# DLRM tower: the turns of gathered rows on VectorE in two pieces of 256 batch columns

## The chip, the cores and the metric

The kernel runs on one core of one Trainium2 chip. The metric is the device time in microseconds (us), from the start of the program on the core to its end. Engines go by the profile's names: PE (TensorE), PEld (its weight loads), DVE (VectorE), ACT (ScalarE), POOL (GpSimd) and SP (SyncE, which issues DMAs here).

## What is computed

For 512 samples, 40 embedding rows of 32 numbers each are looked up; each of the 780 pairs of fields gives one bilinear number; these and 16 dense numbers go through a three-layer perceptron.

```python
e = jnp.stack([tbl_0[ids[:, 0]], ..., tbl_39[ids[:, 39]]], axis=1)   # (512, 40, 32)
xi = inputs[:, iidx, :]          # inputs is e; iidx, jidx = triu_indices(40, k=1)
xj = inputs[:, jidx, :]
out = jnp.einsum('bpd,pde,bpe->bp', xi, bilinear_matrices, xj)      # z, (512, 780)
h = jnp.concatenate([z, dense_ctx], axis=1)
h = jnp.maximum(h @ W_top1 + b_top1, 0.0)    # 796 -> 512
h = jnp.maximum(h @ W_top2 + b_top2, 0.0)    # 512 -> 256
y = h @ W_top3                               # (512, 1)
```

## The kernel before

The fields stand in ten groups of four. A group's embeddings lie in `xt[:, t, :]` with the batch along the free dimension: 4 fields x 32 numbers on 128 partitions, 512 batch columns. They come there in two ways. Four groups (`HOT_POS` = 0, 1, 3, 5) have small tables; PE picks their rows by one-hot matmuls in the first 35 us. The other six (`GATHER_POS` = 2, 4, 6, 7, 8, 9) are gathered by GpSimd: sixteen indirect DMAs a group, each for 32 samples, into `x_rows[:, g, c, :]`, batch along the partitions. A **turn** is the 32x32 block transpose on DVE (L498) that makes `xt[:, t, :]` from `x_rows[:, g]`. It waits for the group's gathers on `gathered[g]` and counts `turned`; PE, DVE and SP wait for a group by that count (`x_there`), and ScalarE waits for the fourth turn before it reuses the first columns of `x_rows`.

The pairs are worked off in 49 **units**, k = 0 to 48 (`UNIT[k] = (t, u)`). A unit is

- on PE, four fp32 matmuls (L564, eight records in the trace) of 32 rows each, which form y = M x in four PSUM banks. They run as two pairs. Each pair takes one of three slots of two banks (`Y_SLOTS` = 3) and waits (`prod_done`) until DVE has read what stood in it: for the first pair of unit k that is product 2 of unit k-2, for the second pair product 1 of unit k-1;
- on DVE, two **products** of 128x1024 elements (L517), y times the partner's embeddings. Product 1 reads the first pair of banks, product 2 the second. Each waits for `y_done`; product 1 of the later units for `sum_done` too, and where t = u for the rearranged rows of `mix_pieces` (`mixed`), which SP moves inside SBUF;
- on PE again, two units later, the **sum** (L635): four matmuls that add each product over its 32 numbers into `z_ps`. Eight units fill a block, which ScalarE copies to `z_t`.

From unit 11 on PE also works at the first layer: one **first-layer half** (L534) of 256 columns a unit, two in units 17, 23, 31 and 39 and none in the units after these. The order on PE within a unit is: the unit's matmuls, the sum of unit k-2, the first-layer half. ScalarE and GpSimd take the results out and add them. After the last unit come the last block's layer, the second and the third layer.

The order of the work is written out in tables. `AFTER["turn"] = [1, 10, 17, 23, 31, 39]` says ahead of which unit's products DVE does each turn; in the code before, a turn stands whole ahead of product 1 of that unit. `LATE_SUMS` puts off the sums of units 0 to 8, so that in unit 10 PE has two sums (7 and 8) and in units 3 to 9 the sum of unit k-3.

Of the kernel before, what the change touches and what calls it, by code (L numbers as in the profile page):

```python
# [44 lines left out]
GATHER_POS = [t for t in range(GROUPS) if t not in HOT_POS]  # L45
GATHERS = len(GATHER_POS)
CHUNKS = BATCH // DIM

# [38 lines left out]
def partner(t, u, s):  # L89

    if t != u:
        return t
    if t % 2 == 0 and s == FREE_ROW[t // 2]:
        return SPLIT[0] if t > 0 else t
    if t % 2 == 1 and s == G - 1:
        return t ^ 1
    return mix_slot(t, s)
# [12 lines left out]
def mix_pieces(g):  # L110

    pieces = []
    for s in range(G):
        if leaves(g, s) is None or (g % 2 == 1 and s == G - 1):
            continue
        for jj, (source, q) in enumerate(leaves(g, s)):
            if jj > 0 and pieces[-1][2] == source and pieces[-1][3] + pieces[-1][4] == q:
                pieces[-1][4] += 1
            else:
                pieces.append([mix_slot(g, s), jj, source, q, 1])  # L120
    return pieces
# [32 lines left out]
L1_HALF = BATCH // 2  # L154
# [8 lines left out]
AFTER = {  # L163
    "l1": sorted([*(k for k in range(11, UNITS) if k - 1 not in TURN_STEPS), *TURN_STEPS, 45, 48]),
    "turn": [1, 10, 17, 23, 31, 39],
}


def place_of(k):
# [36 lines left out]
def bass_dlrm_tower(nc, ids, rows, hot_ids, numbers, negatives, hot_tables, dense, mats, w1, b1, w2, b2, w3, select, out):  # L206
    steps = schedule()

    def x_there(engine, t):

        if t in HOT_POS:
            engine.wait_ge(x_out, 2 * HOT_POS.index(t) + 2)
        else:
            engine.wait_ge(turned, GATHER_POS.index(t) + 1)
# [4 lines left out]
    with ExitStack() as ctx:  # L219
        def sb(name, shape, dt=F32):  # L220
            return ctx.enter_context(nc.sbuf_tensor(name, shape, dt))
# [4 lines left out]
        def sem(name):  # L226
            return ctx.enter_context(nc.semaphore(name))

        ids_sb = sb("ids_sb", [P, 2, GATHERS * CHUNKS], I32)
        row = sb("row", [P, GATHERS * CHUNKS], I32)  # L230
        x_rows = sb("x_rows", [P, GATHERS, CHUNKS, DIM])
        xt = sb("xt", [P, GROUPS + 3 * 2 * MIX_RING, BATCH])
# [32 lines left out]
        def ones(j):  # L265

            if j in BY_SCALAR:
                n = 2 * (scalar_rounds.index(j) % ONES_RING)
                return z_t[:, 1 + n:3 + n, :].rearrange("p b c -> p (b c)").bitcast(BF16).rearrange(
                    "p (f c) -> p f c", f=G)  # L270
            return hot[:, vector_rounds.index(j) % HOT_RING, :, :]
# [29 lines left out]
        w1_rest_in = sem("w1_rest_in")  # L301
        head_in = sem("head_in")
        w2_in = sem("w2_in")
        gathered = [sem(f"gathered{g}") for g in range(GATHERS)]
        mats_in = [sem(f"mats_in{c}") for c in range(len(MAT_CHUNKS))]
        plane_done = [sem(f"plane_done{o}") for o in range(HOTS)]
        hot_done = sem("hot_done")
# [1 line left out]
        turned = sem("turned")  # L309
# [21 lines left out]
        @block.gpsimd  # L331
        def _(pool):
            pool.wait_ge(ids_in, 16)
            nc.gpsimd.tensor_tensor(row[:], ids_sb[:, 0, :], ids_sb[:, 1, :], ALU.add).then_inc(row_done, 1)
            pool.wait_ge(row_done, 1)
            for g in range(GATHERS):
                for c in range(CHUNKS):
                    n = g * CHUNKS + c
                    pool.indirect_dma_start(out=x_rows[:, g, c, :], out_offset=None, in_=rows,  # L339
                                            in_offset=bass.IndirectOffsetOnAxis(ap=row[:, n:n + 1], axis=0)  # L340
                                            ).then_inc(gathered[g], 16)
            for n, (b, m) in enumerate(L1_STEP):
                if b > 1:
                    pool.wait_ge(t_out, n + 1)
                    if b > 2:
                        pool.wait_ge(joined, L1_STEP.index((b - 1, m)) - M1 + 1)
                    nc.gpsimd.tensor_tensor(h1[:, m, :], part_sb[b][:, m * BATCH:(m + 1) * BATCH], h1[:, m, :],  # L347
                                            ALU.add).then_inc(joined, 1)
# [131 lines left out]
        @block.vector  # L480
        def _(dve):
            nc.vector.memset(prod[:, 0, 0, :], 0.0).then_inc(cleared, 1)  # L482
            dve.wait_ge(number_in, 16)
            for k in range(len(ROUND)):
                o, r = ROUND[k]
                if r == 0:
                    dve.wait_ge(hot_id_in[o], 16)
                if k not in BY_SCALAR:
                    n = vector_rounds.index(k)
                    if n >= HOT_RING:  # L490
                        dve.wait_ge(hot_used, vector_rounds[n - HOT_RING] + 1)
                    nc.vector.tensor_scalar(ones(k).rearrange("p f b -> p (f b)"), hot_id[:, o, :],  # L492
                                            number[:, o, r:r + 1], None, ALU.is_equal).then_inc(hot_done, 1)
            for k in range(UNITS):
                for g in [g for g, before in enumerate(AFTER["turn"]) if before == k]:
                    t = GATHER_POS[g]
                    dve.wait_ge(gathered[g], 16 * CHUNKS)
                    nc.vector.transpose(xt[:, t, :], x_rows[:, g, :, :].rearrange("p c d -> p (c d)")).then_inc(turned, 1)  # L498
                t, u = UNIT[k]
                if u != t and all(v == w or v != t for v, w in UNIT[:k]):  # L500
                    x_there(dve, t)
                if u == t:
                    dve.wait_ge(mixed[t], 16 * len(mix_pieces(t)))
                    x_there(dve, t ^ 1)
                    if t % 2 == 0 and t > 0:
                        x_there(dve, SPLIT[0])
                    pairs = [sorted(partner(t, u, s) for s in (2 * half, 2 * half + 1)) for half in range(2)]
                    partners = [xt[:, low:high + 1:high - low, :] for low, high in pairs]
                else:
                    partners = [xt[:, t, :].unsqueeze(1).to_broadcast([P, 2, BATCH])] * 2  # L510
                for half in range(2):
                    slot = (2 * k + half) % Y_SLOTS
                    dve.wait_ge(y_done, 2 * k + half + 1)
                    if half == 0 and k >= PROD_UNITS:

                        dve.wait_ge(sum_done, k - PROD_UNITS + 1)
                    nc.vector.tensor_tensor(prod[:, k % PROD_UNITS, 2 * half:2 * half + 2, :],  # L517
                                            y_ps[:, 2 * slot:2 * slot + 2, :], partners[half],
                                            ALU.mult).then_inc(prod_done, 1)
            dve.wait_ge(sum_done, UNITS)  # L520
            nc.vector.tensor_copy(z_t[:, BLOCKS - 1, :], z_ps[:]).then_inc(z_last, 1)
            for m in range(M1):
                dve.wait_ge(joined, L1_STEP.index((BLOCKS - 2, m)) - M1 + 1)
                dve.wait_ge(l1_done, m + 1)
                nc.vector.tensor_tensor(h1[:, m, :], y_ps[:, LATE_BANK[m], :], h1[:, m, :], ALU.add).then_inc(l1_added, 1)

        @block.tensor
        def _(pe):
# [17 lines left out]
            def first_steps(k):  # L546

                nonlocal chunks_seen
                t, u = UNIT[k]
                if MAT0[chunks_seen] <= k:  # L550
                    pe.wait_ge(mats_in[chunks_seen], 16)
                    chunks_seen += 1
                if all(w != u for _, w in UNIT[:k]):
                    x_there(pe, u)
                for s in range(G):
                    half = 2 * k + s // 2
                    slot = half % Y_SLOTS
                    if s % 2 == 0 and half >= Y_SLOTS:

                        pe.wait_ge(prod_done, half - Y_SLOTS + 1)  # L560
                    elif s % 2 == 0:
                        pe.wait_ge(x_out, 2 * half + 2)
                    rows = slice(s * DIM, (s + 1) * DIM)
                    last = nc.tensor.matmul(y_ps[:, 2 * slot + place(t, u, s) % 2, :], m_sb[rows, k, :], xt[rows, moving(t, u, s), :],  # L564
                                            start=True, stop=True)
                    if s % 2 == 1:
                        last.then_inc(y_done, 1)
# [178 lines left out]
```

## Time and profile before

| | us |
|---|---|
| median of 3 runs | 171.64 (171.23 to 171.9) |
| the profiled execution | 171.2 |
| its span | 169.4 |
| PE busy | 164.5 (97%) |
| DVE busy | 145.0 (86%) |
| POOL busy | 112.8 (67%) |
| ACT busy | 42.8 (25%) |

The span is the time from the first to the last instruction of the profiled execution; 1.8 us of that execution lie around it. A row of the timeline gives start, duration, engine, line, operation, tiles and how many instructions follow each other without a gap; the bracket gives the idle time ahead and what ended it. PE's matmuls overlap, so in the chain of waits a group counts from where the one ahead of it ended. The granted clock of TensorE is at full speed throughout the span (1.00 in the mean).

### The profile page before, as it was taken

What the parts mean: (1) busy time and instruction counts of PE and PEld (TensorE: products, weight loads), DVE (VectorE), ACT (ScalarE), POOL (GpSimd) and SP (SyncE); (2) the same over time, 40 slices, a digit from 0 to 9 for tenths busy, and PEclk for the clock granted to TensorE, in tenths of its full rate; (3) what the DMA queues carried; (4) which work ended last, traced back from release to release, by engine and by line L of the source; (5) the groups of instructions that cost most, each with busy time, mean ns of one, the idle gap of its engine ahead of it and who ended that gap; (6) DMA issues with size and microseconds to landing.
All of it is one profiled execution on the core that took longest, in us unless ns stands there. A gap on an engine that the chain in (4) does not pass through costs nothing.

```text
span 169.4 us, 3937 instructions
## 1 busy us (share of the span) xinstructions
PE 164.5 (97%) x1670; PEld 53.0 (31%) x1670; DVE 145.0 (86%) x144; ACT 42.8 (25%) x56; POOL 112.8 (67%) x117
## 2 busy tenths in 40 slices
PE   6999999999999999999999999999999999999993
PEld 2334444332232223333232223332323323232220
DVE  1799999999999999999999899998999999793500
ACT  3389995120000011130020210202111021111503
POOL 3777777777777777777777777777799993333000
PEclk9999999999999999999999999999999999999999
DMA  5999156987998570100026611000003450000000
GB/s 134 374 423 376 30 151 201 316 245 220 307 360 276 153 220 16 15 12 16 16 52 179 174 23 16 16 14 13 16 12 93 119 164 2 4 0 0 4 0 0
DMA packets 12890, 20.15 MB, mean 119 GB/s; under 512 B 3924, under 2 KB 6872, under 8 KB 12744
## 3 DMA queue, kind: packets, MB, share of 16 engines
q1 hardware_dynamic: 9144, 18.03, 32.7%
q0 software_dynamic: 3072, 1.58, 5.7%
q10 hardware_dynamic: 656, 0.28, 0.6%
q8 instruction: 13, 0.21, 0.5%
q14 instruction: 5, 0.04, 0.1%
HBM read 11.92 MB, written 0.00 MB: 70 GB/s over the span
## 4 chain that ended last, share of the span: by engine, by line
PE 87%; ACT 4%; DMA 4%; issue 2%; SPq 1%
PE y_ps L564 33%; PE z_ps L635 29%; PE t_ps L534 10%; PE y_ps L534 6%; DMA table<-hot_tables 4%; PE y_ps L578 4%; PE t_ps L578 3%; ACT plane L414 2%; PE z_ps L578 1%; ACT z_t L424 1%; PE y_ps L543 1%; SPq L356 1%; ACT xt L433 0%; ACT hot_id L475 0%; ACT xt L435 0%
## 5 line engine op out<-in xcount | busy, mean ns | idle before, releaser
L517 DVE TENSOR_TENSOR prod<-y_ps,xt 128x1024 f32<-128x1024 f32 x98 | 114.4, 1217 | 6.2 <-PE y_ps L564 3.2
L339 POOL DMA_INDIRECT x_rows<-rows,row x96 | 92.3, 961 | 29.2 <-issue 28.9
L564 PE MATMUL y_ps<-xt,m_sb 32*128 32x512 f32 x392 | 60.0, 640 | 0.0
L635 PE MATMUL z_ps<-prod,sel 128*32 128x512 f32 x392 | 51.8, 604 | 0.0
L564 PEld LDWEIGHTS y_ps<-xt,m_sb 32*128 32x128 f32 x392 | 19.1, 182 | 25.7 <-issue 16.7
L492 DVE TENSOR_SCALAR hot<-hot_id,number 128x2048 bf16<-128x2048 int16 x34 | 22.9, 749 | 4.2 <-DMA hot_id<-hot_ids 4.1
L534 PE MATMUL t_ps<-z_t,table 128*32 128x256 f32 x320 | 23.5, 379 | 0.0
L635 PEld LDWEIGHTS z_ps<-prod,sel 128*32 128x32 f32 x392 | 7.9, 107 | 36.3 <-DVE prod L517 17.3
L534 PEld LDWEIGHTS t_ps<-z_t,table 128*32 128x32 f32 x320 | 10.4, 110 | 21.4 <-issue 20.4
L578 PE MATMUL y_ps<-hot,plane 128*32 128x512 bf16 x200 | 15.1, 379 | 0.4 <-ACT plane L414 0.4
L461 ACT ACTIVATE z_t<-z_ps 128x512 f32<-128x512 f32 x6 | 3.6, 597 | 38.9 <-PE z_ps L635 38.9
L347 POOL TENSOR_TENSOR hot_id<-x_rows,hot_id 128x512 f32<-128x512 f32 x4 | 5.1, 1274 | 9.8 <-ACT x_rows L458 9.8
L458 ACT ACTIVATE hot<-t_ps 128x512 f32<-128x512 f32 x8 | 4.8, 596 | 22.7 <-PE t_ps L534 22.7
L414 ACT ACTIVATE plane<-table 128x512 bf16<-128x512 uint8 (+2 forms) x10 | 9.1, 966 | 3.9 <-DMA table<-hot_tables 3.9
L347 POOL TENSOR_TENSOR hot_id<-hot,hot_id 128x512 f32<-128x512 f32 x8 | 9.9, 1273 | 0.0
L578 PE MATMUL y_ps<-hot,table 128*32 128x512 bf16 x100 | 9.7, 383 | 0.2 <-DVE hot L492 0.2
L534 PE MATMUL y_ps<-hot_id,w_sb 128*32 128x512 f32 x64 | 7.0, 592 | 0.0
L572 PE MATMUL y_ps<-prod 128*128 128x512 bf16 x14 | 5.5, 576 | 1.5 <-DVE prod L482 1.5
L578 PEld LDWEIGHTS y_ps<-hot,plane 128*32 128x32 bf16 x200 | 5.2, 97 | 4.8 <-ACT plane L414 0.9
L454 ACT ACTIVATE hot_id<-t_ps,b_sb 128x512 f32<-128x512 f32 x4 | 2.7, 687 | 15.4 <-PE t_ps L534 15.4
L458 ACT ACTIVATE x_rows<-t_ps 128x512 f32<-128x512 f32 x4 | 2.4, 597 | 13.5 <-PE t_ps L534 13.5
L578 PE MATMUL t_ps<-hot,plane 128*32 128x512 bf16 x72 | 5.3, 380 | 0.0
(41 smaller groups left out, 58.5 us busy)
## 6 DMA issues: line engine op xcount, KB each, us to landing
xt<-xt SPq DMA_DIRECT2D x18, 192.0 KB, 2.5
xt<-xt SPq DMA_DIRECT2D x17, 128.0 KB, 2.4
hot_id<-hot_ids SPq DMA_DIRECT2D x4, 512.0 KB, 6.0
xt<-xt SPq DMA_DIRECT2D x32, 64.0 KB, 2.3
x_rows<-rows,row POOLq DMA_INDIRECT x96, 2.4
table<-hot_tables SPq DMA_DIRECT2D x2, 640.0 KB, 8.5
table<-w SPq DMA_DIRECT2D x1, 1280.0 KB
table<-hot_tables SPq DMA_DIRECT2D x2, 512.0 KB, 6.0
```

The lines of the kernel that those rows point to most:

```text
L339: pool.indirect_dma_start(out=x_rows[:, g, c, :], out_offset=None, in_=rows, in_offset=bass.IndirectOffsetOnAxis(ap=row[:, n:n + 1], axis= ...
L347: nc.gpsimd.tensor_tensor(h1[:, m, :], part_sb[b][:, m * BATCH:(m + 1) * BATCH], h1[:, m, :], ALU.add).then_inc(joined, 1)
L414: nc.scalar.activation(plane[:, o % PIECE_RING, byte, :, cols], low_byte(table[:, o, :, :], byte)[:, :, cols], ACT.Copy, scale=256.0 if by ...
L458: nc.scalar.activation(part_sb[b][:, m * BATCH:(m + 1) * BATCH], t_ps[:], ACT.Copy).then_inc(t_out, 1)
L461: nc.scalar.activation(z_t[:, k, :], z_ps[:], ACT.Copy).then_inc(z_out, 1)
L492: nc.vector.tensor_scalar(ones(k).rearrange("p f b -> p (f b)"), hot_id[:, o, :], number[:, o, r:r + 1], None, ALU.is_equal).then_inc(hot_ ...
L517: nc.vector.tensor_tensor(prod[:, k % PROD_UNITS, 2 * half:2 * half + 2, :], y_ps[:, 2 * slot:2 * slot + 2, :], partners[half], ALU.mult). ...
L534: last = nc.tensor.matmul(bank[q * DIM:(q + 1) * DIM, :], weights[:, q * DIM:(q + 1) * DIM], columns, start=start, stop=stop, skip_group_c ...
L564: last = nc.tensor.matmul(y_ps[:, 2 * slot + place(t, u, s) % 2, :], m_sb[rows, k, :], xt[rows, moving(t, u, s), :], start=True, stop=True)
L572: nc.tensor.matmul(y_ps[:, 0, :], zeros[:, BATCH:BATCH + P], zeros[:, 0:BATCH], start=True, stop=True)
L578: done = nc.tensor.matmul(bank[f * DIM:(f + 1) * DIM, :], piece[:, f, r * DIM:(r + 1) * DIM], ones(j)[:, f, :], start=first, stop=last, sk ...
L635: last = nc.tensor.matmul(z_ps[s * DIM:(s + 1) * DIM, :], window, prod[:, k % PROD_UNITS, place(*UNIT[k], s), :], start=first, stop=(k == ...
```

## The change

Each turn is cut into two pieces of 256 columns. The gathers of a group count on two semaphores, one for its first eight and one for its last eight, and each piece waits for its own. The second piece stands where the turn stood; the first stands one unit earlier, except in the turn ahead of unit 1, whose two pieces both stand there. `turned` is counted by the second piece alone.

```diff
+HALF_CHUNKS = CHUNKS // 2
...
+TURN_BEFORE = {}
+for g, k in enumerate(AFTER["turn"]):
+    for half in range(2):
+        TURN_BEFORE.setdefault(k - (half == 0 and k > 1), []).append((g, half))
...
-        gathered = [sem(f"gathered{g}") for g in range(GATHERS)]
+        gathered = [[sem(f"gathered{g}_{half}") for half in range(2)] for g in range(GATHERS)]
...
-                                            ).then_inc(gathered[g], 16)
+                                            ).then_inc(gathered[g][c // HALF_CHUNKS], 16)
...
-                for g in [g for g, before in enumerate(AFTER["turn"]) if before == k]:
-                    t = GATHER_POS[g]
-                    dve.wait_ge(gathered[g], 16 * CHUNKS)
-                    nc.vector.transpose(xt[:, t, :], x_rows[:, g, :, :].rearrange("p c d -> p (c d)")).then_inc(turned, 1)
+                for g, half in TURN_BEFORE.get(k, []):
+                    chunks = slice(half * HALF_CHUNKS, (half + 1) * HALF_CHUNKS)
+                    dve.wait_ge(gathered[g][half], 16 * HALF_CHUNKS)
+                    turn = nc.vector.transpose(xt[:, GATHER_POS[g], half * L1_HALF:(half + 1) * L1_HALF],
+                                               x_rows[:, g, chunks, :].rearrange("p c d -> p (c d)"))
+                    if half == 1:
+                        turn.then_inc(turned, 1)
```

`L1_HALF` is 256. Nothing else is changed; the other engines have the same instructions in the same order.

On DVE, units 9 and 10 before (L517 the products, L498 the turn):

```order
L517 TENSOR_TENSOR prod<-y_ps,xt 128x1024 [waits sum_done,y_done]
L517 TENSOR_TENSOR prod<-y_ps,xt 128x1024 [waits y_done]
L498 STREAM_TRANSPOSE xt<-x_rows 128x512 [waits gathered1]
L517 TENSOR_TENSOR prod<-y_ps,xt 128x1024 [waits sum_done,y_done]
L517 TENSOR_TENSOR prod<-y_ps,xt 128x1024 [waits y_done]
```

The same place after (L526 the products, L504 the turn's pieces; `gathered1_0` and `gathered1_1` are the semaphores of its first and last eight gathers):

```order
L504 STREAM_TRANSPOSE xt<-x_rows 128x256 [waits gathered1_0]
L526 TENSOR_TENSOR prod<-y_ps,xt 128x1024 [waits sum_done,y_done]
L526 TENSOR_TENSOR prod<-y_ps,xt 128x1024 [waits y_done]
L504 STREAM_TRANSPOSE xt<-x_rows 128x256 [waits gathered1_1]
L526 TENSOR_TENSOR prod<-y_ps,xt 128x1024 [waits sum_done,y_done]
L526 TENSOR_TENSOR prod<-y_ps,xt 128x1024 [waits y_done]
```

The turn stood between the products of unit 9 and those of unit 10; a first piece now stands ahead of unit 9's.

On DVE, units 16 and 17 before; unit 16 is one with t = u, whose product 1 has four waits:

```order
L517 TENSOR_TENSOR prod<-y_ps,xt 128x1024 [waits y_done,sum_done,turned,mixed5]
L517 TENSOR_TENSOR prod<-y_ps,xt 128x1024 [waits y_done]
L498 STREAM_TRANSPOSE xt<-x_rows 128x512 [waits gathered2]
L517 TENSOR_TENSOR prod<-y_ps,xt 128x1024 [waits sum_done,y_done,turned]
L517 TENSOR_TENSOR prod<-y_ps,xt 128x1024 [waits y_done]
```

The same place after:

```order
L504 STREAM_TRANSPOSE xt<-x_rows 128x256 [waits gathered2_0]
L526 TENSOR_TENSOR prod<-y_ps,xt 128x1024 [waits y_done,sum_done,turned,mixed5]
L526 TENSOR_TENSOR prod<-y_ps,xt 128x1024 [waits y_done]
L504 STREAM_TRANSPOSE xt<-x_rows 128x256 [waits gathered2_1]
L526 TENSOR_TENSOR prod<-y_ps,xt 128x1024 [waits sum_done,y_done,turned]
L526 TENSOR_TENSOR prod<-y_ps,xt 128x1024 [waits y_done]
```

Again one piece has moved ahead of the two products of the unit before, unit 16. The products that follow the pieces wait for the same semaphores as before.

## Rows read from the trace of the kernel before

**Rows 1.** busy by stretch: window, us, busy (count) of PE, PEld, DVE, ACT, POOL
```profile
55.00:152.00 97.00, 97.00 (x924) 29.80 (x920) 91.12 (x81) 14.06 (x24) 71.52 (x71) 1.00 0.23 59
```

**Rows 2.** chain of waits, 52 to 60 us: start us, us, what
```profile
52.76 1.85 PE z_ps L635 x16
54.61 1.07 PE y_ps L564 x8
...
57.11 1.07 PE y_ps L564 x8
58.18 1.00 PE z_ps L635 x8
59.18 0.43 PE t_ps L534 x8
```

**Rows 3.** timeline, DVE, 50.5 to 56: start, us, what, count [idle before]
```profile
50.36 2.34 DVE L517 TENSOR_TENSOR prod<-y_ps,xt 128x1024 f32<-128x1024 f32 x2
52.62 0.70 DVE L498 STREAM_TRANSPOSE xt<-x_rows 128x512 f32<-128x512 f32 x1
53.25 2.31 DVE L517 TENSOR_TENSOR prod<-y_ps,xt 128x1024 f32<-128x1024 f32 x2
55.77 1.22 DVE L517 TENSOR_TENSOR prod<-y_ps,xt 128x1024 f32<-128x1024 f32 x1 [0.21 <-issue]
```

**Rows 4.** timeline, DVE, 65.9 to 75, read in four pieces
```profile
65.90 2.36 DVE L517 TENSOR_TENSOR prod<-y_ps,xt 128x1024 f32<-128x1024 f32 x2 [0.34 <-PE y_ps L564]
68.38 2.35 DVE L517 TENSOR_TENSOR prod<-y_ps,xt 128x1024 f32<-128x1024 f32 x2
70.65 0.70 DVE L498 STREAM_TRANSPOSE xt<-x_rows 128x512 f32<-128x512 f32 x1
71.38 2.36 DVE L517 TENSOR_TENSOR prod<-y_ps,xt 128x1024 f32<-128x1024 f32 x2
73.77 1.23 DVE L517 TENSOR_TENSOR prod<-y_ps,xt 128x1024 f32<-128x1024 f32 x1
```

**Rows 5.** timeline, PE, L564 of units 10, 17 and 18
```profile
51.42 1.33 PE L564 MATMUL y_ps<-xt,m_sb 32*128 32x512 f32 x8
...
69.67 1.14 PE L564 MATMUL y_ps<-xt,m_sb 32*128 32x512 f32 x8
...
72.60 1.20 PE L564 MATMUL y_ps<-xt,m_sb 32*128 32x512 f32 x8
```

**Rows 6.** chain of waits, 69 to 94 us
```profile
69.74 1.07 PE y_ps L564 x8
...
74.79 1.39 PE y_ps L564 x8
...
77.61 1.07 PE y_ps L564 x8
...
85.10 1.07 PE y_ps L564 x8
...
93.12 1.07 PE y_ps L564 x8
```

**Rows 7.** groups by line: count | busy us, mean ns | idle before, releaser
```profile
L517 DVE TENSOR_TENSOR prod<-y_ps,xt 128x1024 f32<-128x1024 f32 x98 | 114.4, 1217 | 6.2 <-PE y_ps L564 3.2 <-issue 0.2
L339 POOL DMA_INDIRECT x_rows<-rows,row x96 | 92.3, 961 | 29.2 <-issue 28.9 <-POOL row L334 0.3
...
L498 DVE STREAM_TRANSPOSE xt<-x_rows 128x512 f32<-128x512 f32 x6 | 4.2, 703 | 0.2 <-DMA x_rows<-rows,row 0.2
```

**Rows 8.** groups by form, DVE: the products of 512 columns
```profile
L525 DVE TENSOR_TENSOR hot_id<-y_ps,hot_id 128x512 f32<-128x512 f32 x4 | 2.8, 692 | 1.9 <-PE y_ps L534 1.9
```

**Rows 9.** timeline, DVE, 28 to 34: the product after the first turn
```profile
31.81 2.36 DVE L517 TENSOR_TENSOR prod<-y_ps,xt 128x1024 f32<-128x1024 f32 x2 [0.15 <-PE y_ps L564]
```

**Rows 10.** timeline, DVE, 82.5 to 87.2: the fourth turn
```profile
86.28 0.71 DVE L498 STREAM_TRANSPOSE xt<-x_rows 128x512 f32<-128x512 f32 x1 [0.22 <-DMA x_rows<-rows,row]
```

## The prediction

> **What bounds the kernel now.** I read the busy times by stretch first, then the chain of waits, then the timelines of VectorE (DVE) and TensorE (PE) around the turns. From 55 to 152 us PE is busy for all 97.0 us and DVE for 91.1 [rows 1]. There the chain consists of PE rows alone: a unit's first matmuls (L564) 1.07, a sum (L635) 1.00, a first-layer half (L534) 0.43, so 2.50 us from one unit to the next [rows 2]. I write U(k) for the L564 group of unit k; the one that the chain has at 54.61 is U(11), at 57.11 U(12), at 69.74 U(17).
>
> Two loops matter. The first is DVE's own pitch: the two products of a unit last 2.34 to 2.36 together and one lasts 1.21 to 1.23 [rows 3, 4], so they start 1.13 to 1.14 apart, so a unit costs DVE 2.27 against PE's 2.50, and DVE has 0.23 free per unit. The second is narrower. The second pair of matmuls in U(k+1) needs the PSUM banks that product 1 of unit k reads. One place shows it: U(10) starts at 51.42 and lasts 1.33, where the undisturbed U(17) lasts 1.14 [rows 5]; its second pair started 0.19 late, at 51.61, and product 1 of unit 9 ended at 51.57 (50.36 plus 1.21 [rows 3]). So PE goes on about 0.05 after that product's end. Round this loop: product 1 of a unit starts 1.17 after the unit's matmuls do (unit 18: 72.60 in PE's timeline, 73.77 in DVE's [rows 4, 5]), it takes 1.23, the release 0.05: 2.45. Against 2.50 that is 0.05 of slack. Where a unit has no first-layer half (unit 18, PE needs 2.07) the loop itself holds PE for 0.3 to 0.4: U(19) lasts 1.39 in the chain, 0.32 over 1.07 [rows 6]. Where a unit has two such halves (17, 23, 31, 39, just where the turns stand) PE needs 2.93, and 0.48 of delay on DVE is free.
>
> **What the change does, part by part.** Six turns of 0.70 [rows 7] become twelve pieces of 256 columns. A 1024-column product takes 1217 ns and a 512-column one 692 [rows 7, 8], so 512 columns are 525 ns and a piece is 703 minus 262, 0.44 us. In engine time: a whole turn takes 0.63 from its start to the next start where the next product doesn't wait for it (52.62 to 53.25 [rows 3]) and 0.73 where it does (70.65 to 71.38 [rows 4]). A piece then takes 0.37 and 0.47. Together 0.84 for 0.73: DVE does 0.1 more per turn. Bounds: the cheapest piece is half a turn with no fixed part (0.28 and 0.38), the dearest costs what a whole one does (0.63 and 0.73). I take 0.37 and 0.47, since the 512- and 1024-column rows show both slope and fixed part.
>
> The Trainium skill (VectorE: DVE Perf Modes, section "The TRN2 errata — SBUF-src ops pay a fixed extra latency per instruction") says that an SBUF-source operation pays a fixed extra cost per instruction, and gives about 151 cycles at 0.96 GHz for fp32; it advises tiles of 512 elements or more. By it a piece is (256 + 151)/0.96, an estimate of 0.42 us, and each added instruction costs 0.16; all six on the path would be 0.9, and the kernel at 172.6. The rows give a similar fixed part (692 minus 525 ns), but the price here is set by place, as follows.
>
> Turn before unit 1 (both pieces stay there): 0.1 more on DVE, which idled 0.15 behind this turn until PE's group for the next product was there [rows 9]. Cover: just that 0.15. Cost 0, at most 0.1.
>
> Turn before unit 10: its first piece now stands ahead of product 1 of unit 9. Up to here DVE runs without a gap, and U(10) waits for just that product [rows 3, 5]. The product ends 0.37 later, and with it U(10). Behind U(10) stand two sums and U(11) without a wait (52.76, 1.85, then 54.61 [rows 2]), so PE is 0.37 late from then on. Before, the whole turn cost nothing: it lay beside these two sums, and DVE even idled 0.21 before 55.77 [rows 3]. Smaller work on DVE there gives nothing back. **+0.37**.
>
> Turn before unit 17: the first piece goes ahead of product 1 of unit 16. Product 2 of unit 15 starts at 67.05 (65.90 plus 1.14), so the piece starts at 68.18 and product 1 of unit 16 at 68.55, not 68.38 [rows 4]; PE's second pair in U(17) comes at 68.55 + 1.23 + 0.05 = 69.83 where it came with the first at 69.67 [rows 5]. **+0.16**. The second piece leaves product 1 of unit 17 at about 71.28, 0.1 earlier, but PE reaches U(18) only after the two first-layer halves. What that takes away is the 0.06 by which U(18) lasted longer than U(17) [rows 5], and nothing comes of it: the next link, from U(18)'s start to U(19)'s second pair, is the 2.45 loop, which begins at PE's own start and not at the turn's end. Before unit 31 the same (unit 30 too is of the kind with several waits): **+0.16**.
>
> Turn before unit 39: unit 38 is a plain one, in the 2.50 rhythm. Of the piece's 0.37 DVE's free 0.23 hides the most; product 1 starts 0.14 late, and the loop becomes 2.45 + 0.14 = 2.59 against 2.50. **+0.09**.
>
> Turn before unit 23: the same +0.09, but here the turn waited 0.22 for its last gather [rows 10], and from U(23) to U(26) it took 8.02 (85.10 to 93.12), from U(17) to U(20) 7.87 (69.74 to 77.61 [rows 6]). With everything before 0.53 late, DVE comes to the second piece after the gather has landed, so 0.15 comes back. **-0.06**.
>
> The semaphore per piece does nothing more: the first eight gathers of a group land some 10 us before the last eight (GpSimd takes 0.96 and 0.30 of idle time for each of the 96 [rows 7], eight are 10 us). Only the second piece counts `turned`, so PE, SP and ScalarE wait for the same point as before; SP's moves after the turn of unit 10 come at most 0.1 later relative to DVE, and their use is a dozen microseconds off. What queues behind each first piece is only DVE's products, and behind them PE.
>
> Sum: 0.37 + 0.16 - 0.06 + 0.16 + 0.09 = **0.72 us**, all in PE's chain, and from unit 40 to the end nothing can take it back. The profiled execution took 171.2 (span 169.4 and 1.8 around it); it would take 171.9. It is 0.4 under the median of the runs shown, 171.64; on that the forecast is 172.3. With the cheap bound the same working gives 0.28 + 0.07 - 0.15 + 0.07 + 0 = 0.3 (171.9), with the dear one 0.63 + 0.49 + 0.27 + 0.49 + 0.42 = 2.3 (173.9).
>
> **Rivals.** (a) *The stall behind each turn goes.* Smaller pieces would leave DVE never more than half a turn behind, and U(18), U(19) and their three fellows would last 1.07. They are 0.37 over it per turn [rows 5, 6], so 4 x 0.37 = 1.5 us, 170.1. For it: these stalls stand right behind the turns, and only there. Against: by DVE's pitch product 1 of unit 18 could have started at 73.66 (71.38 plus twice 1.14 [rows 4]), and it started at 73.77, when U(18), 72.60 plus 1.20, was nearly through. It decides if U(19) falls from 1.39 to under 1.15. A half case of it (0.3 to 0.8 gained, at unit 23 above all, where DVE was late) would be within 0.5%.
> (b) *A piece costs nearly a whole turn*, by a wait before each or a fixed part larger than in products: up to 2.3, 173.9; half way 173.1. For it: no 256-column operation stands in the trace. Against: the fixed part of two lengths agrees with that of the turn.
> (c) *The change doesn't bite*: the piece before unit 9 finds a gap, or the waiting product starts sooner behind it than I think: 0 to 0.3, 171.8.
> (d) *The mix transfers of groups 4 and 5 become late*, since `turned` comes later: against it, the transfers land well before units 15 and 16. Under 3 in 100.
>
> **How the numbers follow.** My case (0.45 to 1.0 slower, 172.1 to 172.6) 0.55; (c) 0.17; (b) with (d) 0.18, 172.6 to 173.9; (a) 0.07 in full and 0.03 in half. What can be told from no change is 0.5%, 0.86 us, so the border is at 172.5. Of my case 0.14 lies over it; with 0.17 of (b) and (d) slower gets 0.31. Faster by over 0.86 is (a) in full, 0.07 and a little, 0.08. The rest is 0.61. The range goes from 171.4 to 173.1: it leaves out (a), the upper half of (b) and the noise of a median whose runs spread over 0.7.
>
> **What would show it.** In the changed profile: twelve transposes of about 0.44; U(10) lasting about 1.7 in PE's timeline where it was 1.33, and U(11) 0.4 later; U(17), U(31) about 0.15 longer, U(23) and U(39) 0.1; U(19) still about 0.3 over; no gather wait before unit 23. The forecast is wrong if a piece takes over 0.55, or if U(19) and its fellows lose their stall.

## The result and the profile after

| | runs | median, us | lowest to highest |
|---|---|---|---|
| before | 16 | 171.55 | 171.17 to 172.05 |
| changed | 16 | 172.02 | 171.57 to 173.34 |

The ratio is 1.0035, with a 95% interval of 1.0021 to 1.0049: the changed kernel takes 0.6 us more, between 0.4 and 0.8. That is beyond the uncertainty of this comparison, and under the 0.5% that the forecast took as the border of no change. The forecast was 172.3, 0.72 us more. The profiled execution took 172.33, its span is 170.5. The ratios here and below leave out three executions of a slower state, one of experiment 1 (175.62) and two of experiment 7 (174.7 and 175.66).

The pieces in DVE's groups by form, which answer to the last of [rows 7] (count, then busy us, mean ns of one, idle before):

```profile
L504 DVE STREAM_TRANSPOSE xt<-x_rows 128x256 f32<-128x256 f32 x12 | 5.1, 428 | 0.0
```

Twelve pieces of 428 ns stand in place of six turns of 703, so 0.9 us more of turning in all, and none of them waited for a gather. The busy time by stretch, columns as in [rows 1]:

```profile
55.00:152.00 97.00, 97.00 (x916) 29.54 (x912) 90.64 (x85) 14.37 (x24) 71.33 (x72) 1.00 0.23 61
```

DVE's 90.64 is under the 91.12 of before although it turns more: the window stands still, and the work in it has moved by 0.7 to 1.2 us, so these two are not the same work. PE has no idle time, as before; what it lost doesn't show as idleness, because a matmul group that waits halfway through counts as busy (the 1.45 at 75.90 below lies in this stretch). It shows in the chain of waits, whose rows answer to [rows 2, 6] (start us, us, what; L573 is the unit's matmuls, L644 the sums, L543 the first layer and, at the end, the last layers):

```profile
49.93 1.30 PE y_ps L573 x8
...
52.23 1.60 PE y_ps L573 x7
...
58.18 1.07 PE y_ps L573 x8
...
70.81 1.16 PE y_ps L573 x8
...
73.83 1.07 PE y_ps L573 x8
...
75.90 1.45 PE y_ps L573 x8
...
78.77 1.07 PE y_ps L573 x8
...
94.17 1.07 PE y_ps L573 x8
...
135.16 1.07 PE y_ps L573 x8
...
156.43 10.48 PE y_ps L543 x96
```

The rows of the chain before that stand beside these and were not shown yet, U(9), U(42) and the last layers:

```profile
49.19 1.31 PE y_ps L564 x8
...
133.98 1.07 PE y_ps L564 x8
...
155.26 10.48 PE y_ps L534 x96
```

Read as distances from U(9): U(12) came 7.92 after it and comes 8.25 after it; U(20) 28.42 and 28.84; U(26) 43.93 and 44.24; U(42) 84.79 and 85.23; the last layers 106.07 and 106.50. The difference grows by 0.33 at unit 10 and 0.09 at 17, falls by 0.11 at 23, and grows by 0.13 at 31 and 39 together (0.09 and 0.04, as U(31) and U(39) are 0.09 and 0.04 longer); nothing comes after U(42). In all it is 0.43. U(9) itself starts 0.74 later than before (49.93 and 49.19), of which more below.

DVE around units 9 to 11 and 16 to 18, which answer to [rows 3, 4]:

```profile
51.10 0.43 DVE L504 STREAM_TRANSPOSE xt<-x_rows 128x256 f32<-128x256 f32 x1
51.46 2.31 DVE L526 TENSOR_TENSOR prod<-y_ps,xt 128x1024 f32<-128x1024 f32 x2
53.70 0.42 DVE L504 STREAM_TRANSPOSE xt<-x_rows 128x256 f32<-128x256 f32 x1
56.84 3.67 DVE L526 TENSOR_TENSOR prod<-y_ps,xt 128x1024 f32<-128x1024 f32 x3 [0.48 <-issue]
...
69.25 0.43 DVE L504 STREAM_TRANSPOSE xt<-x_rows 128x256 f32<-128x256 f32 x1
69.60 2.31 DVE L526 TENSOR_TENSOR prod<-y_ps,xt 128x1024 f32<-128x1024 f32 x2
72.30 2.35 DVE L526 TENSOR_TENSOR prod<-y_ps,xt 128x1024 f32<-128x1024 f32 x2
```

The piece at 51.10 holds product 1 of unit 9 back to 51.46; with U(9) at 49.93 that is 1.53 behind it, where it had been 1.17 (50.36 [rows 3] and 49.19). Behind the second piece DVE now idles 0.48 ahead of 56.84, where it idled 0.21: its time was free there, and the change took it where it was not. PE's groups of units 10 and 17, which answer to [rows 5]:

```profile
52.16 1.67 PE L573 MATMUL y_ps<-xt,m_sb 32*128 32x512 f32 x8
...
70.74 1.23 PE L573 MATMUL y_ps<-xt,m_sb 32*128 32x512 f32 x8
```

U(10) lasts 1.67 instead of 1.33, U(17) 1.23 instead of 1.14.

### The profile page after: what moved, and what is told of

It reads as the page before. It is cut to its first block, busy times and chain, and to the rows that moved or that the text cites. A ratio compares the mean times of both kernels' runs of the same rounds, so it can differ in the third digit from the quotient of the medians.

```text
span 170.5 us, 3943 instructions
## 1 busy us (share of the span) xinstructions
PE 164.6 (97%) x1670; PEld 53.7 (32%) x1670; DVE 145.0 (85%) x150; ACT 42.8 (25%) x56; POOL 113.4 (66%) x117
## 4 chain that ended last, share of the span: by engine, by line
PE 87%; DMA 4%; ACT 4%; issue 2%; SPq 1%
PE y_ps L573 33%; PE z_ps L644 28%; PE t_ps L543 10%; PE y_ps L543 6%; DMA table<-hot_tables 4%; PE y_ps L587 4%; PE t_ps L587 3%; ACT plane L420 2%; PE z_ps L587 1%; ACT z_t L430 1%; PE y_ps L552 1%; SPq L362 1%; ACT xt L439 0%; ACT hot_id L481 0%; ACT xt L441 0%
## 5 line engine op out<-in xcount | busy, mean ns | idle before, releaser
L526 DVE TENSOR_TENSOR prod<-y_ps,xt 128x1024 f32<-128x1024 f32 x98 | 114.4, 1216 | 6.6 <-PE y_ps L573 4.0
L573 PE MATMUL y_ps<-xt,m_sb 32*128 32x512 f32 x392 | 60.5, 640 | 0.0
L644 PE MATMUL z_ps<-prod,sel 128*32 128x512 f32 x392 | 51.8, 604 | 0.0
L573 PEld LDWEIGHTS y_ps<-xt,m_sb 32*128 32x128 f32 x392 | 19.1, 183 | 26.1 <-issue 16.7
L498 DVE TENSOR_SCALAR hot<-hot_id,number 128x2048 bf16<-128x2048 int16 x34 | 22.9, 748 | 5.1 <-DMA hot_id<-hot_ids 4.7
L543 PE MATMUL t_ps<-z_t,table 128*32 128x256 f32 x320 | 23.5, 379 | 0.0
L644 PEld LDWEIGHTS z_ps<-prod,sel 128*32 128x32 f32 x392 | 7.9, 108 | 36.3 <-DVE prod L526 17.4
L543 PEld LDWEIGHTS t_ps<-z_t,table 128*32 128x32 f32 x320 | 10.4, 110 | 21.4 <-issue 20.4
L543 PE MATMUL y_ps<-hot_id,w_sb 128*32 128x512 f32 x64 | 7.1, 592 | 0.0
```

The costliest lines, as they stand in the source:

```text
L543: last = nc.tensor.matmul(bank[q * DIM:(q + 1) * DIM, :], weights[:, q * DIM:(q + 1) * DIM], columns, start=start, stop=stop, skip_group_c ...
L644: last = nc.tensor.matmul(z_ps[s * DIM:(s + 1) * DIM, :], window, prod[:, k % PROD_UNITS, place(*UNIT[k], s), :], start=first, stop=(k == ...
```

## The experiments

Experiments 1 to 4 and 5 to 8 were timed in two series of five rounds, 9 in three rounds, each beside the kernel before on the same chip (ten to twelve executions of each, seven of experiment 6); 10 and 11 ran once, for their traces. A few tenths of a microsecond are near what such a comparison resolves, so each is read in its trace too: the distance from U(9) to the last layers, 106.07 before and 106.50 in the changed kernel. Ahead of U(9) only the turn at unit 1 is changed, and U(1) to U(9) takes 18.59 in both (30.60 to 49.19, 31.34 to 49.93).

| kernel | ratio to before (95%) | U(9) to last layers | against before |
|---|---|---|---|
| changed | 1.0035 (1.0021 to 1.0049) | 106.50 | +0.43 |
| 1: unit 10's pieces together | 0.9981 (0.996 to 1.0003) | 106.17 | +0.10 |
| 2: all pieces in the turn's place | 0.9973 (0.995 to 0.9995) | 105.93 | -0.14 |
| 3: first piece between the products | 0.9988 (0.9963 to 1.0013) | 105.93 | -0.14 |
| 4: changed, one first-layer half a unit | 0.998 (0.9959 to 1.0001) | 105.96 | -0.11 |
| 5: before, one first-layer half a unit | 1.0031 (1.002 to 1.0043) | 106.58 | +0.51 |
| 6: pieces placed one by one | 0.9961 (0.9948 to 0.9974) | 105.44 | -0.63 |
| 7: before, unit 10's turn whole at unit 9 | 1.0023 (1.0007 to 1.0038) | 106.52 | +0.45 |
| 8: changed, once more | 1.0021 (0.9995 to 1.0046) | 106.50 | +0.43 |
| 9: before, start delayed | 1.0011 (0.9994 to 1.0028) | 105.91 | -0.16 |
| 10: experiment 2 once more | one run | 105.93 | -0.14 |
| 11: before once more | one run | 106.74 | +0.67 |

The last three show that the kernel before has no single distance: with no wait for a gather it is 105.91 (experiment 9, whose added operation lies ahead of U(9)), with the 0.22 of the first profile 106.07, with one of 0.88 it is 106.74. The changed kernel had no such wait in either profile. So the column is best read against 105.91, and the changed kernel's own cost is 0.59. The timed ratios of experiments 1 to 4 lie 0.1 to 0.4 us lower than this column. Longer waits of the kernel before in that series would do it, but no trace of that series' kernel before was taken, so this stays open.

**Experiment 1.** The two pieces of unit 10's turn together, the other four as changed.

```diff
-        TURN_BEFORE.setdefault(k - (half == 0 and k > 1), []).append((g, half))
+        TURN_BEFORE.setdefault(k - (half == 0 and k > 10), []).append((g, half))
```

> Both pieces of the turn ahead of unit 10 stand at unit 10; the other four keep their first piece a unit earlier. Theory (a first piece costs what it delays product 1 of a unit whose product PE's next pair of matmuls waits for): the group of unit 10 lasts as in the kernel before, unit 11 comes at the kernel before's distance, and 0.33 us of the changed kernel's loss is gone: about 0.1 us over the kernel before (171.7). Rival (the loss is spread over all turns, one piece more each at 0.1 us): a gain of no more than 0.05 on the changed kernel. Rival (the loss is in the start of the program, which came 0.74 us later in the changed kernel's profile): no gain at all.

Its chain of waits, U(9), U(10) and the last layers:

```profile
49.57 1.30 PE y_ps L573 x8
...
51.87 1.27 PE y_ps L573 x8
...
155.74 10.48 PE y_ps L543 x96
```

U(10) is back at 1.27, and 0.33 of the 0.43 is gone. One piece of 0.43 us ahead of one product makes three quarters of the loss. The timed runs agree in direction: 171.42 beside 171.74 for the kernel before in the same series, while the changed kernel is over it. Its median is under that of the kernel before, although its trace is 0.10 longer; the interval holds 1, and the varying wait of experiments 9 to 11 may account for the rest.

**Experiment 2.** Every turn split, nothing moved ahead.

```diff
-        TURN_BEFORE.setdefault(k - (half == 0 and k > 1), []).append((g, half))
+        TURN_BEFORE.setdefault(k, []).append((g, half))
```

> Both pieces of every turn stand where the turn stood, so the turns are split and nothing is moved ahead. Theory (splitting costs nothing by itself, place does): no delay at units 10, 17, 31 and 39, and at unit 23 only the second piece (0.47) instead of the whole turn (0.73) stands behind the last gather, which gives 0.15: 0.15 us under the kernel before, 171.4. Rival (each piece more costs 0.1 to 0.16 us on the path): 0.4 to 0.8 us over the kernel before.

Its chain, and DVE at unit 23:

```profile
49.67 1.31 PE y_ps L573 x8
...
155.60 10.48 PE y_ps L543 x96
```

```profile
86.47 0.76 DVE L504 STREAM_TRANSPOSE xt<-x_rows 128x256 f32<-128x256 f32 x2
```

0.14 under before, the interval just clear of 1. So splitting costs nothing, though DVE does as much as in the changed kernel. The 0.14 are the gather wait at unit 23, which isn't there: the turn before started at 86.28, after 0.22 of idle time [rows 10]; here both pieces follow the products at once, at 86.47. But this program reached U(9) 0.48 later than the one before, so a whole turn wouldn't have waited either; what the split does for it is left to experiments 9 to 11.

**Experiment 3.** The first piece a unit ahead, but behind product 1 of that unit.

```diff
+for g, k in enumerate(AFTER["turn"]):
+    TURN_BEFORE.setdefault((k - 1, 1) if k > 1 else (k, 0), []).append((g, 0))
+    TURN_BEFORE.setdefault((k, 0), []).append((g, 1))
...
                 for half in range(2):
+                    if half == 1:
+                        pieces(1)
                     slot = (2 * k + half) % Y_SLOTS
```

> The first piece stands a unit ahead as in the changed kernel, but between product 1 and product 2 of that unit and not ahead of product 1. VectorE's work and nearly its time are those of the changed kernel. Theory (only product 1 is waited for within the 0.05 us of slack; product 2 has over 1 us): no delay of unit 11, none at 17, 31 and 39, the gather gain at 23: 0.13 us under the kernel before. Rival (VectorE's longer way through a unit is what costs): as the changed kernel, 0.4 to 0.6 over the kernel before.

DVE around units 9 and 10, and the chain:

```profile
51.86 0.44 DVE L506 STREAM_TRANSPOSE xt<-x_rows 128x256 f32<-128x256 f32 x1
52.22 1.19 DVE L532 TENSOR_TENSOR prod<-y_ps,xt 128x1024 f32<-128x1024 f32 x1
```

```profile
49.55 1.31 PE y_ps L579 x8
...
155.48 10.48 PE y_ps L549 x96
```

Product 2 of unit 9 starts at 52.22 and is 0.36 late, as product 1 was in the changed kernel, and PE loses nothing. This is the experiment that tells place from amount: one product further, the same piece costs 0.57 us less in all (106.50 and 105.93). Its timed ratio alone doesn't separate it from the kernel before (0.9963 to 1.0013); it lies under the interval of the changed kernel's first comparison (1.0021 to 1.0049).

**Experiment 4.** The changed kernel with the first layer spread evenly.

```diff
-    "l1": sorted([*(k for k in range(11, UNITS) if k - 1 not in TURN_STEPS), *TURN_STEPS, 45, 48]),
+    "l1": sorted([*range(11, UNITS), 45, 48]),
```

> The changed kernel with one first-layer half in every unit from 11, also in 17, 23, 31, 39 (two there before) and 18, 24, 32, 40 (none there before). Theory (the stall of 0.3 to 0.4 us in the second unit behind a turn comes from the unit without a first-layer half, whose own loop is 2.45 us, not from the turn): these four stalls go, and in the units with the second piece a stall of about 0.3 comes up, because their 0.43 of cover is gone; in sum about 0.5 us under the changed kernel and 0.1 under the kernel before. Rival (the turn makes these stalls): they stay at 0.3 us and the units with the turn get 0.4 us longer: over 1 us slower than the changed kernel.

Its chain, U(9), U(18), U(19) and the last layers:

```profile
49.88 1.30 PE y_ps L573 x8
...
73.35 1.31 PE y_ps L573 x8
...
76.08 1.07 PE y_ps L573 x8
...
155.84 10.48 PE y_ps L543 x96
```

U(19), which lasted 1.45, lasts 1.07: the stall in the second unit behind the turn was that of the unit without a first-layer half, and it goes when the half is put there. U(18) takes over 0.24 of it (1.31), the second piece's share. In sum 0.54 us under the changed kernel. Rival (a), that the turn itself makes that stall, is refuted from both sides: smaller turns left it (1.45), and the even schedule removed it with the pieces in the same places.

**Experiment 5.** The same edit in the kernel before, with whole turns.

> The kernel before, turns whole and in their old places, with one first-layer half in every unit from 11 on (none doubled at the turns). Theory: a whole turn makes product 1 of its unit 0.55 late, and with no second first-layer half to cover it PE waits 0.5 for it, while the stall of the unit without a half (0.37) goes: about 0.1 worse per turn, 0.45 us over the kernel before. With the last experiment this shows where pieces a unit apart pay: in such a schedule they are 0.5 us better than whole turns, in the old one 0.4 worse. Rival (pieces a unit apart are worse in any schedule): this one is faster than the fourth experiment.

```profile
49.11 1.30 PE y_ps L564 x8
...
72.16 1.55 PE y_ps L564 x6
...
155.69 10.48 PE y_ps L534 x96
```

U(18) lasts 1.55, the 0.5 that a whole turn costs without the second half's cover, and U(19), next in that chain, 1.07. In this schedule whole turns are 0.62 us worse than pieces a unit apart (106.58 and 105.96), of which some 0.26 stands at unit 23, where the turn waited 0.20 for its gather (its U(24) lasts 1.81, not 1.55); in the old one they were 0.43 better, 0.59 without a gather wait. The two edits belong together, and the change made one of them. Both together, which is experiment 4, come out even with the kernel before without a wait: 105.96 and 105.91.

**Experiment 7.** The kernel before with unit 10's turn whole ahead of unit 9.

```diff
-    "turn": [1, 10, 17, 23, 31, 39],
+    "turn": [1, 9, 17, 23, 31, 39],
```

> The kernel before with one number changed: the turn ahead of unit 10 stands whole ahead of unit 9. Theory (PE is late by what stands ahead of product 1 of unit 9, here 0.63 instead of the 0.36 of a piece): unit 11 comes 0.60 later, 0.15 of it comes back at the gather of unit 23, 0.45 us over the kernel before. Rival (one piece or turn at this place costs a fixed wait, whatever its length): 0.33 as for the piece.

```profile
49.54 1.30 PE y_ps L564 x8
...
51.84 1.86 PE y_ps L564 x8
...
156.06 10.48 PE y_ps L534 x96
```

U(10) lasts 1.86, 0.59 over 1.27, where the piece made it 1.60. So the price at this place follows the length of what stands there. The sum is +0.45, the 0.15 at unit 23 having come back as with the piece. Its U(9) stood 0.35 later than before, so the 0.59 at unit 10 was not alone in bringing DVE to that turn behind its gather.

**Experiment 8.** The changed kernel once more.

> The changed kernel once more, for two things. From unit 2 to unit 48 the distance should again be 0.44 us over the kernel before's trace, term by term as in the first profile. The start of unit 1, which was 0.73 us later in the changed kernel's profile than in the one before, should lie anywhere in the 0.3 to 0.8 that the other profiles showed, if it hangs on when the first transfers land and not on the change; if the six more semaphores delay it, it is 0.7 again and the other split kernels, with the same semaphores, would have shown it too.

```profile
30.57 1.07 PE y_ps L573 x8
...
49.15 1.30 PE y_ps L573 x8
...
155.65 10.48 PE y_ps L543 x96
```

106.50 again, to the hundredth, now with U(9) as early as in the kernel before (49.15 and 49.19), so the distance doesn't hang on the late start of the first profile. The timed ratio of this second comparison, 1.0021, is smaller than the first and its interval just holds 1. U(1) starts at 30.57 here; in the first profile of the changed kernel it was 31.34, in the one of before 30.60, in the others 30.52 to 31.09, but for experiment 9, where it was delayed. The late start of the first profile is thus not the change's. DVE waited 4.70 us for the first indices in that profile and 4.06 in the one before, and these 0.64 make up most of the 0.74.

**Experiments 9, 10 and 11.** The gather wait, in three runs: the kernel before with a delayed start, experiment 2's kernel and the kernel before once more.

```diff
                 columns = ones(j).rearrange("p f b -> p (f b)")
+                if n == 0:
+                    nc.scalar.activation(y[:].bitcast(BF16), hot_id[:, o, 0:2 * P], ACT.Abs, bias=negative[:, n:n + 1])
```

> The kernel before, with one small ScalarE operation of 256 columns added in the start (its result is overwritten before use), which delays unit 0 by 0.3 to 0.4 us. GpSimd's gathers start from other transfers and aren't delayed. The second experiment's 0.14 was read as the split's, but its units started 0.48 later than those of the kernel before, so a whole turn would not have waited for its gather there either. Theory (the wait is a race between the start and GpSimd's gathers): the distance from U(9) to the last layers is 105.92 to 105.98 instead of 106.07, and the whole kernel only 0.2 slower. Rival (the split gives it): 106.07 as before.

> The second experiment's kernel once more, for its start. If U(9) comes as early as in the kernel before (49.2), theory: the second piece starts with the last gather or 0.1 before VectorE's own time, and the distance is still 105.93, so that the split keeps the gather wait off in an early start. Rival: 106.07, the split gives nothing there.

> The kernel before once more, for its start: with U(9) at 49.2 the distance is 106.07, with U(9) 0.2 or more later it is 105.92 (between them, in between). Rival (the gather wait is there whatever the start): 106.07 in any case.

U(9) and the last layers in the chain of experiment 9:

```profile
50.45 1.30 PE y_ps L566 x8
...
156.36 10.48 PE y_ps L536 x96
```

of experiment 10, with the turn of unit 23 on DVE:

```profile
49.22 1.31 PE y_ps L573 x8
...
155.15 10.48 PE y_ps L543 x96
```

```profile
86.02 0.77 DVE L504 STREAM_TRANSPOSE xt<-x_rows 128x256 f32<-128x256 f32 x2
```

and the same of experiment 11:

```profile
49.15 1.30 PE y_ps L564 x8
...
155.89 10.48 PE y_ps L534 x96
```

```profile
86.91 0.71 DVE L498 STREAM_TRANSPOSE xt<-x_rows 128x512 f32<-128x512 f32 x1 [0.88 <-DMA x_rows<-rows,row]
```

With the start delayed (by more than I meant: U(9) at 50.45), the whole turn had no wait for a gather in the trace and the distance is 105.91, as the theory had it. With the early start of experiment 10 (U(9) at 49.22, the 64th gather at 83.91) the split kernel doesn't wait either, 105.93: the pieces go from 86.02 on without a gap, where the whole turn of the first profile could go only at 86.28. The rival, 106.07, is refuted, though by one execution. Experiment 11 missed its number: U(9) stood at 49.15 as in the first profile, and the distance is 106.74, since the turn waited 0.88, and U(24) lasted 2.07 in its chain. GpSimd was late itself: the start of its 64th gather, the last of this group, lay at 84.58 there, at 83.88 in the first profile and between 83.85 and 84.31 in the others. So the wait depends on two things that vary from execution to execution, when the units start and how fast the gathers go.

**Experiment 6.** A version made from what experiments 1 to 4 had shown: each piece where DVE's free time covers it, and the first layer's halves one a unit but for units 23 and 24; of the two left over at the end one moves from unit 45 to 47.

```diff
-    "l1": sorted([*(k for k in range(11, UNITS) if k - 1 not in TURN_STEPS), *TURN_STEPS, 45, 48]),
+    "l1": sorted([*(k for k in range(11, UNITS) if k != 24), 23, 47, 48]),
...
+PIECES_AT = {1: [(1, 0), (1, 0)], 10: [(10, 0), (10, 0)], 17: [(16, 0), (16, 1)], 23: [(22, 0), (23, 0)],
+             31: [(29, 0), (31, 0)], 39: [(37, 0), (39, 0)]}
```

(unit of the turn: for each piece the unit and whether it stands ahead of product 1 or of product 2)

> Pieces of 256 columns, each put where VectorE's free time covers it: both at unit 10; at unit 16 ahead of product 1 and of product 2; units 22 and 23; 29 and 31; 37 and 39. One first-layer half a unit from 11, two in units 23, 47 and 48, none in 24. Theory (PE waits only for product 1, 0.05 us of slack, 0.23 us free a unit; a piece takes 0.36): summed link by link, 0.7 us under the kernel before, 170.9. Rival (pieces only ever add work): at or over the kernel before.

Its chain, and the second piece of unit 23 on DVE:

```profile
49.40 1.30 PE y_ps L581 x8
...
154.84 10.48 PE y_ps L551 x96
```

```profile
86.51 0.45 DVE L508 STREAM_TRANSPOSE xt<-x_rows 128x256 f32<-128x256 f32 x1 [0.34 <-DMA x_rows<-rows,row]
```

170.75 beside 171.52, a ratio of 0.9961: it beats the kernel before by 0.7 us (0.4 to 0.9) and so the changed one by over 1 us. The trace has 0.63 of the 0.7 expected, and 0.47 against the 105.91 without a gather wait. At unit 23 the piece waited 0.34 for its gather and U(24) lasts 1.32; from U(23) to U(26) it takes 7.98, where the same stretches from U(17), U(31) and U(39) take 7.68, 7.71 and 7.64. How much of that is the wait and how much the old doubled half, which stayed at this place alone, wasn't tried. DVE was ready for the piece at 86.17, no sooner than for the turn of the first profile (86.06), but the 64th gather began at 84.16 and not at 83.88. So this execution met a late gather; that GpSimd's pace is the next limit here is likely, and not shown.

## Why the prediction was right, point by point

- *Which way and how much.* 0.72 slower was forecast; measured is 0.6 (0.4 to 0.8) by the runs and 0.43 by the pair of profiles. The case called likeliest, 0.45 to 1.0, holds the first and just misses the second. The second comparison (experiment 8) has 0.4, with an interval from nothing to 0.8. The terms below were all somewhat too high, so that the first comparison comes as near to 0.72 as it does is in part luck.
- *A piece takes 0.44 us, 0.37 to the next start.* 428 ns, and 0.36 (51.10 to 51.46). The fixed part that the Trainium skill gives for fp32 additions (VectorE: DVE Perf Modes, "The TRN2 errata — SBUF-src ops pay a fixed extra latency per instruction") led to an estimate of 0.42, and the trace agrees: 703 minus 428 is 275 ns for 256 columns, which leaves 153 ns. Its advice of 512 elements and more holds for the engine's time; in experiment 2 following it would have gained nothing, since the extra time fell where DVE had some left.
- *Unit 1, nothing.* It was nothing: U(1) to U(9) takes 18.59 in both kernels.
- *Unit 10, +0.37.* It was 0.33, and the mechanism is shown: experiments 1 and 3 take the loss away by moving the piece from ahead of product 1 of unit 9 to behind it, experiment 7 scales it with the length.
- *Units 17 and 31, +0.16 each; unit 39, +0.09; unit 23, -0.06.* They were 0.09, 0.09, 0.04 and -0.11. All four, and unit 10, are 0.04 to 0.07 too high: the mis-sized part is the product's length in the loop. I let product 1 behind a piece last 1.23. It lasts 1.18 or 1.19 when it doesn't wait for the piece (experiment 3's row at 52.22 for product 2; in the changed kernel the pair at 51.46 lasts 2.31 and not 2.35), and frees its banks 0.04 sooner. The kernel before already showed it: in [rows 3] the pair at 53.25 lasts 2.31, and I read only its start. The lengths fit each term; no run changed the product's length by itself.
- *The gather at unit 23 gives 0.15 back.* It did, and in experiment 8 too, whose start was early. My reason, that DVE comes later, is one of two: experiments 7 and 9 show that a late enough whole turn doesn't wait, but experiment 10 shows that the split alone keeps the wait off, with nothing late. Which of the two did it in the changed kernel can't be told, since it has both.
- *The stalls behind the turns stay (against rival a).* U(19) went from 1.39 to 1.45 and U(18) from 1.12 to 1.07, as the working had it; experiments 4 and 5 show the cause.
- *Rival (b), a dear piece, and (c), a change that doesn't bite,* fell with 0.43 us a piece and with the 0.33 at unit 10. (d): no wait for a mix transfer appeared at units 15 and 16.
- *The dear bound, 2.3.* By the steps of the working a piece of 0.63 gives 0.63 + 0.42 + 0.20 + 0.42 + 0.35 = 2.0; I had 0.07 more at each of the last four. It bore only on how far rival (b) reaches.
- *Base.* I put the shift on the median of three, 171.64; that of sixteen is 171.55.
- *What the sum is set against.* I took the 0.22 of gather wait in one profile for the kernel's own. It varies: 0.22, 0.88 and, with a delayed start, none in three profiles of the same schedule. Against a run without it the change costs 0.33 + 0.09 + 0.04 + 0.09 + 0.04 = 0.59 (106.50 against 105.91), which is also what the sixteen runs show (0.6). How often the kernel before waits, and for how long, wasn't measured, so the agreement is not a proof.

## What to carry to other kernels

Find which of two like instructions the bottleneck waits for before moving work ahead of either: here 0.36 us ahead of the first product cost 0.33, and the same ahead of the second nothing. Split work in its old place cost nothing here. Spread out, it goes together with the schedule of the cover: whole blocks want a doubled filler beside them, pieces an even one. Either edit alone lost 0.4 to 0.6 us, both came out even with a kernel before that doesn't wait for a gather, and with each piece placed by itself 0.7 was won in the timed runs (0.47 by the trace without that wait). Compare traces from an event behind the start-up, whose 0.8 us of spread would have hidden or doubled the effect, and don't take a wait seen in one profile for a constant when its two sides are set by different engines.

## What the runs showed of the hardware that was not expected

A DVE product issued right behind a transpose on which it doesn't wait ends sooner than one behind another product: 1.18 to 1.19 us from start to end instead of 1.21 to 1.23, be it behind a whole turn (at 53.25 before, 1.18) or a piece (52.22 in experiment 3). Why was not tried. And GpSimd's indirect DMAs, issued 1.25 us apart, reached the 64th between 83.85 and 84.58 us in thirteen executions of nearly the same program; the longest single one took 1.09 to 1.47 us.
